# Attention and experts on one core: the softmax shifts turned by VectorE in 32x32 blocks and set in line through memory, in place of TensorE's transposes

## The chip, the cores and the metric

The kernel runs on one core of one Trainium2 chip. Its time is the device time in microseconds (us) of one execution. Five engines of the core matter, each with its own instruction stream: TensorE (PE, with its weight loads PEld), VectorE (DVE), ScalarE (ACT), GpSimd (POOL) and SyncE (SP), which here only waits and issues DMAs. They meet by semaphores.

## The reference

What must be computed, for `x` of shape (4, 2048, 256), float32:

```python
x = x + ln(attn(ln(x)))        # 16 heads of 16, causal
x = x + ln(ffn(ln(x)))         # 8 experts, the 2 best of each batch by its first token

# attn
scores = jnp.where(causal, einsum('bhqd,bhkd->bhqk', q, k) * HD ** -0.5, -inf)
out = einsum('bhqk,bhkd->bhqd', softmax(scores), v)
# ffn
h = gelu(einsum('bsd,bkde->bkse', x, W1[idx]) + b1[idx])
out = sum(einsum('bkse,bkef->bksf', h, W2[idx]) + b2[idx]) / 2
```

## The kernel before, in words

Three stages follow each other. **Stage A** (0 to 207 us) normalises x in 16 chunks of 512 tokens, multiplies by the weights of queries, keys and values, splits queries and keys into three bf16 parts each, and stores all to memory. **Stage B** (207 to 1688 us) is the attention. **Stage C** is the output projection, the layer norms and the experts.

**Stage B's work.** Heads are taken in groups of four, two groups (`g`) in each of eight rounds (`it`). Queries go in four chunks (`c`) of 512, keys in tiles (`kt`) of 128; a *key step* j is one key tile of one chunk of one group, and there are 640. For each step, for each pair of heads (`s`) and each head of the pair (`p`):

- *Scores*, line 1104 (`take_scores`): keys stand still, queries move, two matmuls (`ab`) of up to 512 columns into `psS`. Their contraction takes 64 rows or 33. Heads 0 and 2 use the upper 64 rows of the array (p = 0), heads 1 and 3 the lower 64 (p = 1), and matmuls in different halves run side by side. The 33rd row of the second matmul is a row of ones in `kT` against a row of `qT` that holds each query's *shift*: minus its largest score. So the shift is subtracted inside the matmul.
- *Exponentials*, line 1068, ScalarE: one instruction for two heads.
- *Mask*, line 1039, GpSimd, on tiles at the diagonal.
- *Values*, line 1121 (`take_values`): four heads in float32 into the four 32-column strips of `psO`. One such block uses all 128 rows.

**The maxima.** The shifts must be known before a chunk's first scores. So TensorE computes the scores of a chunk once more, queries standing still, in *units* of up to 512 keys (`multiply`, lines 613 and 615; 613 lays the causal mask down) into a ring of three banks, and VectorE takes each unit's maximum (`reduce`, line 631) and frees the bank. Units with `heads` even use the upper half of the array, odd ones the lower. At the end of a chunk (`ends`) VectorE reduces the parts to `nmax` (line 636): 128 queries by 16 columns (4 heads x 4 tiles). Queries run along partitions there, but the row of `qT` needs them along one partition.

**The turn.** Hence a turn for each chunk, 64 in all, 62 of them in stage B: TensorE transposes `nmax` into a ring bank (line 623), VectorE copies it as bf16 to `nmT` (line 646), and SyncE lays it into rows 32 and 96 of `qT` with four DMAs (`place`, line 653). Scores of the chunk wait for all four (`nm_ld`).

**What sets the order.** `ORDERS` is a string that fixes the order on TensorE for stage B: 0 and 1 are a score matmul for p = 0 or 1, a and b a unit for the upper or lower half, v a block of values, t a turn. VectorE, ScalarE and SyncE walk the same list and pick out their own. The first 54 entries of the list of units (`LEAD`) are done in stage A, two at a time. `PBUF` lets scores run at most four steps ahead of values. SyncE's queue in stage B also holds the loads of the next group (two a step in steps 2 to 14 of each group), and the stores of `outT`.

## Time and profile before

| | |
|---|---|
| median of 3 runs | 2049.87 us (2047.66 to 2054.5) |
| the profiled execution | 2049.51 us |
| its span, first to last instruction | 2047.8 us |
| granted TensorE clock, mean | 0.99 of full speed |
| TensorE busy | 1976.5 us, 97% |
| VectorE busy | 1791.3 us, 87% |
| ScalarE busy | 1363.0 us, 67% |

A busy share is that of an engine over the whole span. Matmuls overlap in the trace, so busy time says that TensorE had something under way, not that it ran at its peak; on TensorE one reads the step from the start of one instruction to the start of the next. A row of weight loads (PEld) that sat idle need not be lost time either, since loads run ahead of matmuls. 1.7 us lie around the span.

### The profile page before, as it was taken

To read this page: it belongs to the slowest core of one execution; us is meant where nothing else is said; L and a number is where in the kernel's file an instruction comes from. 1 tells how busy PE (TensorE), PEld (TensorE's weight loads), DVE (VectorE), ACT (ScalarE), POOL (GpSimd) and SP (SyncE) were. 2 spreads that over 40 slices of the span, in tenths; PEclk is the share of its full clock that TensorE was granted. 3 is DMA by queue.
4 is the path that set the end of the run, shared out by engine and by line. 5 is a ranking of instruction groups with operands and counts; after the bars stand their busy time and mean duration, and the time that the engine had idled before them with its cause. 6 is when DMAs were issued, how large, how long until landed. Compare 5 with 4: busy or idle time off the path is not lost.

```text
span 2047.8 us, 39736 instructions
## 1 busy us (share of the span) xinstructions
PE 1976.5 (97%) x15772; PEld 869.5 (42%) x15772; DVE 1791.3 (87%) x3564; ACT 1363.0 (67%) x1653; POOL 305.4 (15%) x373
## 2 busy tenths in 40 slices
PE   9999999999999999999999999999999996999996
PEld 6655333333333333333333333333333324667664
DVE  6876999999999999989999999999899917898883
ACT  5766757777777777777777777777777781333332
POOL 4333101011010101011010101111010104322000
PEclk9999999999999999999999999999999997999999
DMA  5877515050322304041423505051332034454320
GB/s 171 259 230 202 111 37 101 7 92 22 79 50 49 74 23 91 8 90 27 77 45 51 91 8 90 7 92 34 67 58 41 17 109 113 116 138 112 91 67 31
DMA packets 144907, 162.44 MB, mean 79 GB/s; under 512 B 52946, under 2 KB 118610, under 8 KB 144722
## 3 DMA queue, kind: packets, MB, share of 16 engines
q1 hardware_dynamic: 137554, 147.26, 31.2%
q0 software_dynamic: 7168, 12.64, 2.8%
q8 instruction: 124, 2.03, 0.4%
q14 instruction: 61, 0.50, 0.1%
HBM read 99.77 MB, written 59.77 MB: 78 GB/s over the span
## 4 chain that ended last, share of the span: by engine, by line
PE 81%; DVE 11%; ACT 4%; issue 2%; DMA 1%; SPq 1%; POOL 0%; ACTq 0%; POOLq 0%; DVEq 0%
PE b_psO L1121 25%; PE b_psS L1104 25%; PE b_ring L615 13%; PE a_psQK L906 6%; DVE b_pmax L631 4%; PE c_psH L1501 3%; PE a_psV L918 3%; PE c_psO L1514 3%; ACT b_prob L1068 2%; PE b_ring L613 1%; PE c_psA L1471 1%; DVE c_ln_x_stats L81 1%; DVE c_attn L105 1%; DVE c_ln_f_stats L81 1%; PE a_psT L881 1%
## 5 line engine op out<-in xcount | busy, mean ns | idle before, releaser
L631 DVE TENSOR_REDUCE b_pmax<-b_ring 128x1 f32<-128x512 f32 (+4 forms) x2284 | 1336.7, 648 | 75.1 <-PE b_ring L615 59.2
L1068 ACT ACTIVATE b_prob<-b_psS 128x1024 f32<-128x1024 f32 (+3 forms) x1280 | 1085.2, 895 | 367.3 <-PE b_psS L1104 362.6
L1104 PE MATMUL b_psS<-g_qT,g_kT 64*128 64x512 bf16 (+6 forms) x5120 | 833.2, 347 | 10.1 <-ACT b_prob L1068 7.2
L615 PE MATMUL b_ring<-g_kT,g_qT 64*128 64x512 bf16 (+2 forms) x2500 | 714.5, 348 | 2.9 <-DVE b_pmax L631 1.5
L1121 PE MATMUL b_psO<-b_prob,g_v 128*32 128x512 f32 (+3 forms) x5120 | 595.0, 540 | 0.3
L1104 PEld LDWEIGHTS b_psS<-g_qT,g_kT 64*128 64x128 bf16 (+1 forms) x5120 | 295.4, 94 | 460.6 <-ACT b_prob L1068 343.4
L1039 POOL TENSOR_SCALAR_AFFINE_SELECT b_prob<-b_prob 128x512 f32<-128x512 f32 x256 | 162.7, 636 | 1315.8 <-ACT b_prob L1068 1315.5
L615 PEld LDWEIGHTS b_ring<-g_kT,g_qT 64*128 64x128 bf16 x2500 | 221.2, 94 | 234.2 <-DVE b_pmax L631 162.4
L613 PE MATMUL b_ring<-later,query_of 64*128 64x128 bf16 x988 | 191.9, 219 | 3.0 <-DVE b_pmax L631 2.4
L1121 PEld LDWEIGHTS b_psO<-b_prob,g_v 128*32 128x32 f32 x5120 | 103.4, 108 | 172.1 <-issue 131.9
L1501 PE MATMUL c_psH<-c_yT,c_w1e 128*128 128x512 f32 x256 | 119.4, 613 | 22.0 <-ACT c_hT L1426 21.7
L906 PE MATMUL a_psQK<-c_cc,a_w 128*128 128x512 f32 x256 | 115.8, 599 | 1.2 <-ACT c_cc L833 1.2
L1514 PE MATMUL c_psO<-c_w2e,c_hT 128*128 128x256 f32 x512 | 113.6, 380 | 1.2 <-DMA c_b2e<-in_L_ffn_b 1.2
L613 PEld LDWEIGHTS b_ring<-later,query_of 64*128 64x128 bf16 x988 | 88.1, 94 | 50.3 <-DVE b_pmax L631 23.8
L1514 PEld LDWEIGHTS c_psO<-c_w2e,c_hT 128*128 128x128 f32 x512 | 96.9, 190 | 20.7 <-issue 5.3
L1501 PEld LDWEIGHTS c_psH<-c_yT,c_w1e 128*128 128x128 f32 x256 | 48.5, 194 | 83.2 <-issue 48.1
L1471 PE MATMUL c_psA<-wo,c_cc 128*128 128x256 f32 x256 | 65.6, 415 | 11.8 <-DVE c_attn L1320 7.0
L96 ACT ACTIVATE c_ln_x_std<-c_ln_x_var,eps 128x4 f32<-128x4 f32 x16 | 4.8, 298 | 103.8 <-DVE c_ln_x_var L93 103.8
L1426 ACT ACTIVATE c_hT<-c_psH,c_b1e 128x512 f32<-128x512 f32 x64 | 42.7, 686 | 44.2 <-PE c_psH L1501 44.0
L906 PEld LDWEIGHTS a_psQK<-c_cc,a_w 128*128 128x128 f32 x256 | 47.2, 190 | 54.6 <-issue 54.0
L1471 PEld LDWEIGHTS c_psA<-wo,c_cc 128*128 128x128 f32 x256 | 52.7, 211 | 21.1 <-issue 11.8
L918 PE MATMUL a_psV<-a_w,c_cc 128*128 128x256 f32 x256 | 58.7, 382 | 0.0
(119 smaller groups left out, 1060.5 us busy)
## 6 DMA issues: line engine op xcount, KB each, us to landing
qk_parts<-a_parts SPq DMA_DIRECT2D x64, 384.0 KB, 4.5
g_qT<-qk_parts SPq DMA_DIRECT2D x184, 128.0 KB, 3.9
g_kT<-qk_parts SPq DMA_DIRECT2D x184, 128.0 KB, 5.1
out_sums<-b_outT SPq DMA_DIRECT2D x64, 256.0 KB, 2.4
v_ones<-a_v SPq DMA_DIRECT2D x16, 544.0 KB, 5.8
g_v<-v_ones SPq DMA_DIRECT2D x32, 272.0 KB, 5.3
a_x<-in_L_attn_x SPq DMA_DIRECT2D x16, 512.0 KB, 5.2
c_x<-in_L_attn_x SPq DMA_DIRECT2D x16, 512.0 KB, 7.3
```

Of the source, the lines that this page charges most:

```text
L613: self.nc.tensor.matmul(to[:, w - P:w], consts.query_of[half:half + HALF, :], consts.later[half:half + HALF, :], start=True, stop=False, s ...
L615: ins_ = self.nc.tensor.matmul(to, groups.qT[own, g, h // 2, 0, t * P:(t + 1) * P], groups.kT[own, g, h // 2, 0, pc * CH:pc * CH + w], sta ...
L631: self.nc.vector.tensor_reduce(pmax[:, c % 2].rearrange("p (h t) n -> p h t n", t=TT)[:, heads[0]:heads[-1] + 1:2, qt, pc], bank[:, 0:k * ...
L906: ins_ = nc.tensor.matmul(psQK[:, i % 2], w[:, t, k, m * P:(m + 1) * P], xT[:, n % 2, k], start=(k == 0), stop=(k == KD - 1))
L918: ins_ = nc.tensor.matmul(psV[:, t], xT[:, n % 2, k, t * P:(t + 1) * P], w[:, 2, k], start=(k == 0), stop=(k == KD - 1))
L1039: nc.gpsimd.affine_select(out=tile, in_=tile, compare_op=ALU.is_ge, fill=0.0, base=0, pattern=[[0, HG], [1, P]], channel_multiplier=-1).th ...
L1068: nc.scalar.activation(prob[:, j % PBUF, 2 * s:2 * s + 2, off:CH], psS[:, 2 * s:2 * s + 2, off:CH], ACT.Exp).then_inc(exp_done, 1)
L1104: ins_ = nc.tensor.matmul(psS[:, 2 * s + p, off:CH], kT[own, g, s, ab, kt * P:(kt + 1) * P], qT[own, g, s, ab, c * CH + off:(c + 1) * CH], ...
L1121: ins_ = nc.tensor.matmul(psO[h * VW:(h + 1) * VW, off:CH], vS[:, g, kt, h * VC:h * VC + VW], prob[:, j % PBUF, h, off:CH], start=(kt == 0 ...
L1471: ins_ = nc.tensor.matmul(psA[:, t], cc[:, c, k, t * P:(t + 1) * P], wo[:, k], start=(k == 0), stop=(k == KD - 1))
L1501: ins_ = nc.tensor.matmul(psH[:, i % 2], w1e[:, e, k, m * P:(m + 1) * P], yT[:, k, c], start=(k == 0), stop=(k == KD - 1))
L1514: ins_ = nc.tensor.matmul(psO[:, t], hT[:, e, m, t * P:(t + 1) * P], w2e[:, e, m], start=(i == 0), stop=(i == 2 * KD - 1))
```

## The change

The turn leaves TensorE and its ring bank. `nmax` becomes bf16 with 32 columns, of which 16 stay zero. When a chunk's maxima end, VectorE itself turns `nmax` with one instruction that transposes each 32x32 block in place of its own: it comes out with 32 queries along the free axis, on 128 partitions (4 blocks x 32 columns). `place` then takes two legs. SyncE stores `nmT` to a scratch in memory (`nm_scr`, 128 runs of 64 bytes) so that there each column's 128 queries stand in line, waits until it has landed, and loads from there with two DMAs, one for each half, in place of four. `ORDERS` has no t, and all of it is drawn up anew, so the places of units, scores and values have all moved; the counts of scores and value blocks are the same. The two turns among the first 54 entries make room for two more units in stage A.

```diff
         self.pmax = ctx.enter_context(nc.sbuf_tensor("b_pmax", [P, 2, HG * TT, NC], F32))
-        self.nmax = ctx.enter_context(nc.sbuf_tensor("b_nmax", [P, 2, HG * TT], F32))
-        self.nmT = ctx.enter_context(nc.sbuf_tensor("b_nmT", [HG * TT, 2, P], BF16))
+        self.nmax = ctx.enter_context(nc.sbuf_tensor("b_nmax", [P, 2, BLOCK], BF16))
+        self.nmT = ctx.enter_context(nc.sbuf_tensor("b_nmT", [P, 2, BLOCK], BF16))
+        self.nmax_set = ctx.enter_context(nc.semaphore("b_nmax_set"))
...
+        self.nc.gpsimd.memset(self.nmax[:, :, :], 0.0).then_inc(self.nmax_set, 1)
         self.nc.gpsimd.memset(self.ones[:, :], 1.0).then_inc(self.ones_set, 1)
...
+BLOCK = 32
 GK = sum(TT * (c + 1) for c in range(NC))
 BK = 2 * GK
...
-    jobs, turns = [], []
-    for it in range(NPAIR):
-        for g in range(2):
-            for c in range(NC):
-                for qt in range(TT):
-                    for pc in range(c + 1):
-                        for heads in units(c, qt, pc):
-                            jobs.append(("max", it, g, c, qt, pc, heads))
-                            if turns and turns[0][0] <= len(jobs) - 2:
-                                jobs.append(turns.pop(0)[1])
-                turns.append((len(jobs), ("turn", it, g, c)))
-    return jobs + [turn for _, turn in turns]
+    return [("max", it, g, c, qt, pc, heads) for it in range(NPAIR) for g in range(2) for c in range(NC)
+            for qt in range(TT) for pc in range(c + 1) for heads in units(c, qt, pc)]
...
 ORDERS = (
-    "a1010b0b1b10b011b01010aava110101aa00a0101v010b0101a1b1010bv0b011b011ab0v1a1a0a00101abvb010ba10101av0b011"
...
+    "b0101ab0a101b0101b0101bb0101b1010a0101v10100b011a1010bav1a0b0101a10av1a10b0a1010av1a100a1010bav0b1a1a101"
...
+        self.nm_turned = sem("b_nm_turned")
+        self.nm_stored = sem("b_nm_stored")
 
     @staticmethod
     def bank(r):
...
-    def turn(self, pe, bank, r, it, g, c):
-        self.wait_bank(pe, r)
-        pe.wait_ge(self.nm_done, it * CHUNKS + g * NC + c + 1)
-        self.nc.tensor.transpose(bank[0:HG * TT, 0:P], self.groups.nmax[:, c % 2], self.consts.ident[:, :]
-                                 ).then_inc(self.ring_full, 1)
-
     def reduce(self, v, bank, r, it, g, c, qt, pc, heads, ends):
         pmax, nmax = self.groups.pmax, self.groups.nmax
         k = len(heads)
...
         if ends:
+            n = it * CHUNKS + g * NC + c + 1
             v.wait_ge(self.ring_free, r + 1)
-            self.nc.vector.tensor_reduce(nmax[:, c % 2], pmax[:, c % 2, :, 0:c + 1], AX.X, ALU.max,
+            self.nc.vector.tensor_reduce(nmax[:, c % 2, 0:HG * TT], pmax[:, c % 2, :, 0:c + 1], AX.X, ALU.max,
                                          negate=True).then_inc(self.nm_done, 1)
-
-    def take_turn(self, v, bank, r, it, g, c):
-        v.wait_ge(self.ring_full, r + 1)
-
-        bg, bc = (g, c - 2) if c >= 2 else (1 - g, c + 2)
-        count = (it + (0 if c < 2 and g == 0 else 1)) * 16 * HG
-        if count > 0:
-            v.wait_ge(self.nm_ld[bg][bc], count)
-        self.nc.vector.tensor_copy(self.groups.nmT[:, c % 2], bank[0:HG * TT, 0:P]).then_inc(self.ring_free, 1)
-
-    def place(self, sp, r, it, g, c):
-
-        sp.wait_ge(self.ring_free, r + 1)
-        for h in range(HG):
-            row = h % 2 * HALF + KB
-            sp.dma_start(self.groups.qT[row:row + 1, g, h // 2, 1, c * CH:(c + 1) * CH]
-                         .rearrange("o (q n) -> o q n", n=P),
-                         self.groups.nmT[h * TT:(h + 1) * TT, c % 2, :]).then_inc(self.nm_ld[g][c], 16)
+            if n <= 2:
+                v.wait_ge(self.groups.nmax_set, 1)
+            v.wait_ge(self.nm_done, n)
+
+            bg, bc = (g, c - 2) if c >= 2 else (1 - g, c + 2)
+            count = (it + (0 if c < 2 and g == 0 else 1)) * 16 * 2
+            if count > 0:
+                v.wait_ge(self.nm_ld[bg][bc], count)
+            self.nc.vector.transpose(self.groups.nmT[:, c % 2], nmax[:, c % 2]).then_inc(self.nm_turned, 1)
+
+    def place(self, sp, it, g, c):
+
+        n = it * CHUNKS + g * NC + c + 1
+        sp.wait_ge(self.nm_turned, n)
+        to = self.nm_scr[c % 2]
+        sp.dma_start(to.rearrange("r b n -> b r n"), self.groups.nmT[:, c % 2]).then_inc(self.nm_stored, 16)
+        sp.wait_ge(self.nm_stored, 16 * n)
+        for p in range(2):
+            row = p * HALF + KB
+            sp.dma_start(self.groups.qT[row:row + 1, g, :, 1, c * CH:(c + 1) * CH],
+                         to[0:HG * TT].rearrange("(s p t) b n -> p s (t b n)", p=2, t=TT)[p:p + 1]
+                         ).then_inc(self.nm_ld[g][c], 16)
 
 
...
-                for r, which in leads_of(n):
-                    if which[0] == "turn":
-                        maxima.place(sp, r, *which[1:])
+                for _, (_, it, g, c, *_, ends) in leads_of(n):
+                    if ends:
+                        maxima.place(sp, it, g, c)
...
-            r = LEAD
             summed = []
             for what, *which in ORDER:
                 if what == "max":
-                    r += 1
-                elif what == "turn":
-                    maxima.place(sp, r, *which)
-                    r += 1
+                    it, g, c, *_, ends = which
+                    if ends:
+                        maxima.place(sp, it, g, c)
...
-                    pe.wait_ge(maxima.nm_ld[g][c], (it + 1) * 16 * HG)
+                    pe.wait_ge(maxima.nm_ld[g][c], (it + 1) * 16 * 2)
...
+    nm_scr = nc.dram_tensor("shifts", (2, BLOCK, P // BLOCK, BLOCK), BF16, kind="Internal").ap()
```

In the rows of order below, an instruction is given by its line, what it writes and reads, its shape and the semaphores it waits for. `b_psS` are scores, `b_ring` the units' banks, `b_psO` the values, `b_nm13` and its like say that the shifts of g = 1, c = 3 lie in `qT`.

VectorE before, where the maxima of the last group's first chunk end (`b_pmax` are the units' maxima):

```order
L631 TENSOR_REDUCE b_pmax<-b_ring 128x1 [waits b_ring_full] x3
L631 TENSOR_REDUCE b_pmax<-b_ring 128x2 [waits b_ring_full]
L631 TENSOR_REDUCE b_pmax<-b_ring 128x1 [waits b_ring_full] x23
L636 TENSOR_REDUCE b_nmax<-b_pmax 128x16 [waits b_ring_free]
L631 TENSOR_REDUCE b_pmax<-b_ring 128x1 [waits b_ring_full] x7
L646 CAST b_nmT<-b_ring 16x128 [waits b_nm10,b_ring_full]
L631 TENSOR_REDUCE b_pmax<-b_ring 128x1 [waits b_ring_full] x2
```

VectorE now, at the same place:

```order
L610 TENSOR_REDUCE b_pmax<-b_ring 128x1 [waits b_ring_full] x3
L610 TENSOR_REDUCE b_pmax<-b_ring 128x2 [waits b_ring_full]
L610 TENSOR_REDUCE b_pmax<-b_ring 128x1 [waits b_ring_full] x23
L616 TENSOR_REDUCE b_nmax<-b_pmax 128x16 [waits b_ring_free]
L626 STREAM_TRANSPOSE b_nmT<-b_nmax 128x32 [waits b_nm10,b_nm_done]
L610 TENSOR_REDUCE b_pmax<-b_ring 128x1 [waits b_ring_full] x11
```

The cast of a turned bank, which stood seven units behind the maxima that it belongs to, is gone; a transpose stands right behind `nmax`, and waits for it.

TensorE before, from the last unit of all (its two matmuls into `b_ring` come first) on, with its turn:

```order
L613 MATMUL b_ring<-later,query_of 128x128 [waits b_ring_free]
L615 MATMUL b_ring<-g_kT,g_qT 128x512
L1104 MATMUL b_psS<-g_qT,g_kT 128x512 [waits b_exp_done]
L1104 MATMUL b_psS<-g_qT,g_kT 128x512 x3
L1104 MATMUL b_psS<-g_qT,g_kT 128x384 [waits b_exp_done]
L1104 MATMUL b_psS<-g_qT,g_kT 128x384 x3
L623 MATMUL b_ring<-ident,b_nmax 16x128 [waits b_nm_done,b_ring_free]
L1104 MATMUL b_psS<-g_qT,g_kT 128x384 [waits b_exp_done]
L1104 MATMUL b_psS<-g_qT,g_kT 128x384 x3
L1121 MATMUL b_psO<-b_prob,g_v 32x512 [waits b_exp_done]
L1121 MATMUL b_psO<-b_prob,g_v 32x512 x3
```

TensorE now, from the last unit on:

```order
L598 MATMUL b_ring<-later,query_of 128x128 [waits b_ring_free]
L600 MATMUL b_ring<-g_kT,g_qT 128x512
L1077 MATMUL b_psS<-g_qT,g_kT 128x384 [waits b_exp_done]
L1077 MATMUL b_psS<-g_qT,g_kT 128x384 x3
L1094 MATMUL b_psO<-b_prob,g_v 32x512 [waits b_exp_done]
L1094 MATMUL b_psO<-b_prob,g_v 32x512 x3
L1077 MATMUL b_psS<-g_qT,g_kT 128x384 [waits b_exp_done]
L1077 MATMUL b_psS<-g_qT,g_kT 128x384 x3
L1077 MATMUL b_psS<-g_qT,g_kT 128x256 [waits b_exp_done]
L1077 MATMUL b_psS<-g_qT,g_kT 128x256 x3
L1094 MATMUL b_psO<-b_prob,g_v 32x512 [waits b_exp_done]
L1094 MATMUL b_psO<-b_prob,g_v 32x512 x3
```

The turn, and its wait for `b_nm_done` amid the scores, are gone. From its last unit to the first scores that wait for `b_nm13`, TensorE had 28 score matmuls, a turn and three blocks of values; now it has 24 score matmuls and six blocks.

SyncE before, at the end of stage A (`g_v` are the values that the first scores wait for too, `a_parts` and `a_v` the chunk stores):

```order
L720 DMA qk_parts<-a_parts 128x3x512 [waits a_low_done]
L720 DMA qk_parts<-a_parts 128x3x512 x3
L299 DMA g_v<-v_ones 128x8x68 x2
L715 DMA v_ones<-a_v 128x4x272 [waits a_v_copied]
L720 DMA qk_parts<-a_parts 128x3x512 [waits a_low_done]
L720 DMA qk_parts<-a_parts 128x3x512 x3
L653 DMA g_qT<-b_nmT 1x4x128 [waits b_ring_free]
L653 DMA g_qT<-b_nmT 1x4x128 x3
```

SyncE now, at the same place:

```order
L704 DMA qk_parts<-a_parts 128x3x512 [waits a_low_done]
L704 DMA qk_parts<-a_parts 128x3x512 x3
L633 DMA shifts<-b_nmT 4x32x32 [waits b_nm_turned]
L637 DMA g_qT<-shifts 1x2x512 [waits b_nm_stored]
L637 DMA g_qT<-shifts 1x2x512
L301 DMA g_v<-v_ones 128x8x68 x2
L699 DMA v_ones<-a_v 128x4x272 [waits a_v_copied]
L704 DMA qk_parts<-a_parts 128x3x512 [waits a_low_done]
L704 DMA qk_parts<-a_parts 128x3x512 x3
```

The shifts of the second chunk have moved ahead of the loads of `g_v`, which now wait behind the landing of the store to `shifts`.

## Rows read from the trace of the kernel before

**Rows 1.** The page: each engine's busy time, its share, its instructions.
```profile
PE 1976.5 (97%) x15772; PEld 869.5 (42%) x15772; DVE 1791.3 (87%) x3564; ACT 1363.0 (67%) x1653; POOL 305.4 (15%) x373
```

**Rows 2.** Windows: stretch, then busy time and (instructions) by engine, clock, DMA.
```profile
207.00:320.00 113.00, 107.54 (x938) 39.22 (x939) 107.83 (x190) 75.35 (x91) 13.34 (x19) 0.97 0.31 66
320.00:1605.00 1285.00, 1277.48 (x12142) 470.88 (x12141) 1218.45 (x2165) 969.23 (x1174) 141.36 (x223) 1.00 0.29 54
1605.00:1648.00 43.00, 42.01 (x388) 14.15 (x390) 37.10 (x63) 34.86 (x44) 5.08 (x8) 1.00 0.05 20
1648.00:1688.00 40.00, 37.28 (x329) 8.61 (x325) 0.55 (x3) 32.93 (x40) 5.08 (x8) 1.00 0.42 138
```

**Rows 3.** VectorE by line, 207 to 1648 us: count, busy, mean, idle before.
```profile
L631 DVE TENSOR_REDUCE b_pmax<-b_ring 128x1 f32<-128x512 f32 (+4 forms) x2284 | 1336.7, 648 | 75.1 <-PE b_ring L615 59.2
L646 DVE CAST b_nmT<-b_ring 16x128 bf16<-16x128 f32 x61 | 16.4, 269 | 0.4 <-PE b_ring L623 0.3
L636 DVE TENSOR_REDUCE b_nmax<-b_pmax 128x16 f32<-128x48 f32 (+3 forms) x61 | 12.1, 198 | 2.1
```

**Rows 4.** Timeline of TensorE: a turn behind a value block (start, length).
```profile
228.26 1.06 PE L1121 MATMUL b_psO<-b_prob,g_v 128*32 128x512 f32 x8
229.28 0.27 PE L623 MATMUL b_ring<-ident,b_nmax 128*16 128x128 f32 x1
229.49 0.39 PE L615 MATMUL b_ring<-g_kT,g_qT 64*128 64x512 bf16 x1
```

**Rows 5.** Timeline of TensorE: a turn amid half-array work.
```profile
543.08 0.37 PE L1104 MATMUL b_psS<-g_qT,g_kT 64*128 64x512 bf16 x1
543.38 0.28 PE L623 MATMUL b_ring<-ident,b_nmax 128*16 128x128 f32 x1
543.59 0.39 PE L1104 MATMUL b_psS<-g_qT,g_kT 64*128 64x512 bf16 x1
```

**Rows 6.** Timeline of TensorE: steps of value blocks and of half-array work.
```profile
705.92 1.07 PE L1121 MATMUL b_psO<-b_prob,g_v 128*32 128x512 f32 x8
706.92 0.28 PE L1104 MATMUL b_psS<-g_qT,g_kT 64*128 64x256 bf16 x1
...
711.62 0.39 PE L1104 MATMUL b_psS<-g_qT,g_kT 64*128 64x512 bf16 x2
711.84 0.38 PE L615 MATMUL b_ring<-g_kT,g_qT 64*128 64x512 bf16 x1
```

**Rows 7.** Waits of TensorE's weight loads, 250 to 1640 us: total, times, longest.
```profile
PEld b_ring L615 <- DVE b_pmax L631: 155.4, 384, 0.9
```

**Rows 8.** TensorE's weight loads of the turns, whole run, by line.
```profile
L623 PEld LDWEIGHTS b_ring<-ident,b_nmax 128*16 128x16 f32 x62 | 5.4, 87 | 31.4 <-DVE b_pmax L631 29.3 <-issue 1.3
```

**Rows 9.** Timeline, all engines: the last shifts, their placing, the next scores.
```profile
1648.09 0.22 DVE L636 TENSOR_REDUCE b_nmax<-b_pmax 128x16 f32<-128x64 f32 x1
...
1648.76 0.28 DVE L646 CAST b_nmT<-b_ring 16x128 bf16<-16x128 f32 x1 [0.45 <-PE b_ring L623]
...
1649.07 2.44 SPq L653 DMA_DIRECT2D g_qT<-b_nmT  x4
...
1654.00 1.05 PE L1104 MATMUL b_psS<-g_qT,g_kT 64*128 64x512 bf16 x8 [0.51 <-ACT b_prob L1068]
```

**Rows 10.** DMA issues: count, KB each, median us from issue to landing.
```profile
g_kT<-qk_parts SPq DMA_DIRECT2D x184, 128.0 KB, 5.1
...
g_v<-v_ones SPq DMA_DIRECT2D x32, 272.0 KB, 5.3
...
inverse_sums<-b_pair_sums SPq DMA_DIRECT2D x8, 64.0 KB, 1.6
...
c_b1e<-in_L_ffn_b SPq DMA_DIRECT2D x8, 1.0 KB, 2.6
```

**Rows 11.** Timeline of SyncE's queue before stage B.
```profile
190.39 2.74 SPq L720 DMA_DIRECT2D qk_parts<-a_parts  x4
193.18 2.41 SPq L299 DMA_DIRECT2D g_v<-v_ones  x2
```

More of the change, by code:

```diff
@@ L404, in first_jobs @@
     jobs = max_jobs()
-    return [job if job[0] == "turn" else (*job, not any(other[:4] == job[:4] for other in jobs[r + 1:]))
-            for r, job in enumerate(jobs[:LEAD])]
+    return [(*job, not any(other[:4] == job[:4] for other in jobs[r + 1:])) for r, job in enumerate(jobs[:LEAD])]
 FIRST_JOBS = first_jobs()
@@ L512, in read_orders @@
     jobs = max_jobs()
-    units_of = [[n for n, job in enumerate(jobs) if job[0] == "max" and job[6][0] % 2 == p] for p in range(2)]
-    turns = [n for n, job in enumerate(jobs) if job[0] == "turn"]
+    units_of = [[n for n, job in enumerate(jobs) if job[6][0] % 2 == p] for p in range(2)]
     left = {}
     for job in jobs:
-        if job[0] == "max":
-            left[job[1:4]] = left.get(job[1:4], 0) + 1
+        left[job[1:4]] = left.get(job[1:4], 0) + 1
     for job in jobs[:LEAD]:
-        if job[0] == "max":
-            left[job[1:4]] -= 1
+        left[job[1:4]] -= 1
     order, at, valued = [], [0, 0], 0
     taken = [sum(n < LEAD for n in units_of[p]) for p in range(2)]
-    turned = sum(n < LEAD for n in turns)
     for sign in "".join(ORDERS):
@@ L538, in read_orders @@
             order.append((*job, left[job[1:4]] == 0))
-        elif sign == "t":
-            job = jobs[turns[turned]]
-            turned += 1
-            assert left[job[1:]] == 0
-            order.append(job)
         else:
@@ L547, in read_orders @@
             valued += 1
-    assert valued == len(KEY_STEPS) and turned == len(turns) and not any(left.values())
+    assert valued == len(KEY_STEPS) and not any(left.values())
     return order
@@ L805, in lead @@
                 for r, which in leads(n, k):
-                    if which[0] == "max":
-                        maxima.reduce(v, ring[:, maxima.bank(r)], r, *which[1:])
-                    else:
-                        maxima.take_turn(v, ring[:, maxima.bank(r)], r, *which[1:])
+                    maxima.reduce(v, ring[:, maxima.bank(r)], r, *which[1:])
             normalise(variance(0), 0)
@@ L1048, in _ @@
                     maxima.reduce(v, ring[:, maxima.bank(r)], r, *which)
-                    r += 1
-                elif what == "turn":
-                    maxima.take_turn(v, ring[:, maxima.bank(r)], r, *which)
                     r += 1
@@ L1132, in _ @@
             for what, *which in ORDER:
-                if what in ("max", "turn"):
+                if what == "max":
                     if r == LEAD:
                         pe.wait_ge(stores.v_copied, B * NC)
-                    if what == "max":
-                        maxima.multiply(pe, ring[:, maxima.bank(r)], r, *which)
-                    else:
-                        maxima.turn(pe, ring[:, maxima.bank(r)], r, *which)
+                    maxima.multiply(pe, ring[:, maxima.bank(r)], r, *which)
                     r += 1
```

169 lines of the change are left out of this document (83 added, 86 removed).

## The prediction

> **What bounds the kernel now.** I read the page's first row, then the busy time by stretch, then VectorE by line, then the timeline of TensorE around single turns, then waits and the DMA queue. The page shows TensorE busy 97% of the span [rows 1]. The stretches [rows 2] cut this up; the change works from 207 to 1688 us. From 320 to 1605 TensorE is busy 1277.5 of 1285 us and VectorE 1218.5 (94.8%): two engines near full, with 7.5 and 66.5 us idle. From 207 to 320, the first group, VectorE is busy 107.8 of 113 us and TensorE waits more (107.5): there the reduces set the pace. After 1648 VectorE has nothing left, and ScalarE and TensorE finish alone. So a microsecond saved on TensorE counts in the long middle only as far as VectorE can keep up. It has some room: 75.1 us idle before its reduces, 59.2 of them waiting for TensorE's units [rows 3]. TensorE waits for VectorE too: its weight loads for units stood 384 times for a bank, 155.4 us in sum, most of it under running matmuls [rows 7]. Neither engine alone is the bound; they lean on each other.
>
> **The turns leave TensorE.** Behind a value block, the block takes 1.02 us to the turn's start and the turn 0.21 us to the next start [rows 4]; a like block without a turn takes 1.00 [rows 6]. So 0.21 us each. Amid half-array work the turn comes 0.30 us after its predecessor and gives way after 0.21 [rows 5], where the like step is 0.22 [rows 6]: 0.08 more. In the order string before, 42 of the 62 turns of stage B stand next to a value block, 20 do not. 62 x 0.21 = 13.0, and 20 x 0.08 = 1.6: 14.6 us, the end from below. From above, the weight loads of the 62 turns found their engine idle for 31.4 us [rows 8], 0.51 each, which would all have to be lost time. A turn also holds one of three banks and makes TensorE wait in order for `nmax`, so something of that is lost; I stay near the timelines, with a fifth of the distance: **18.0 us**, 0.29 each.
>
> The Trainium skill has a rule here (TensorEngine Tiling (Array Packing), Key Properties): a change of tiling mode drains the array. Read strictly, each turn would cost its own 0.27 and the drain of its predecessor, 0.17, 62 x 0.44 = 27 us. The rows agree only amid half-array work, and for less; behind value blocks 1.02 against 1.00 shows no drain beyond what a block already pays. By the rule the result would be 9 us lower.
>
> **The halves are filled less evenly.** The new order could give some of this back. Between two value blocks, TensorE needs about as long as the fuller half has columns. Counted over all score and mask and unit matmuls between blocks, the fuller halves hold 1,811,072 columns before and 1,821,056 now; the sum of both halves is the same. At 0.22 us for 512 [rows 6] 9,984 more columns are 4.3 us if the fuller half sets each step. It does so only partly, since other waits cover it; from below it costs nothing. I take **+3**.
>
> **The first group.** There VectorE is the bound, so TensorE's four turns (0.29 x 4) bring nothing by themselves. But until the last value block of that group VectorE takes 173 units in place of 179, counted from both orders; two units went to stage A, where VectorE has room, four to later. At 1336.7 / 2284 = 0.585 us [rows 3] 6 x 0.585 = 3.5, and four casts change for transposes, below, 0.3: **-3.8**. The 58 other turns then count for 18.0 x 58 / 62 = **-16.8**. The last group has 68 units in place of 60, where VectorE has room (37.1 of 43 us [rows 2]) and then nothing.
>
> **VectorE.** 61 casts go, 0.27 each by mean [rows 3]. A transpose of 128x32 bf16 the trace doesn't show. Its nearest rows are the 16-column reduce to `nmax`, 0.20, and the cast, 0.27 [rows 3]; from below half of the former, 0.10, from above twice the latter, 0.54. I take 0.20, with no gap of note before it, since `nmax` itself waits for a reduce in the same way and sat idle 2.1 us over 61 [rows 3]. So VectorE gets 0.07 x 56 = 4 us less to do from 320 to 1605 (from +15 to -10). TensorE wants to be some 13 us quicker there, so VectorE's idle time would shrink from 66.5 to about 57. Less slack means more bank waits; in the trace about 7.5 of TensorE's middle is open idle time with 66.5 of slack, and I give back **+2** (0 to 6). The transpose also stands at once behind its `nmax`; behind it waits the next reduce, and TensorE for its bank, 0.2 us as with the cast.
>
> **The longer way of the shifts.** Now: end of `nmax` to the first issue 0.76 us, four issues to 1651.51, next scores at 1654.00 [rows 9]. New: transpose 0.25 with its wait, issue and landing of the store, issue of two loads (0.6 each, 2.44 / 4 in [rows 9]), landing of the second. A landing isn't shown for such small pieces. Nearest rows: 1.6 us for a 64 KB store, 2.6 for a 1 KB load, 5.1 for a load in the phases when the next group comes in [rows 10]. That makes 0.3 + 1.6 + 0.6 + 2.6 = 5.1 us at best, about 6.5 as I take it, 11 in the loading phases. How much is there? I added the durations of what stands in the new order from a chunk's last unit to its first scores. Of the 62 chunks nine have under 9 us: 3.5, 6.4, 7.0, 7.3, 7.5, 7.8, 7.9, 8.5, 8.7; the other third chunks have 15 and more, second ones 25, first ones 34. All but one are the last chunks of a group, whose maxima end outside the loading phase (steps 2 to 14). The 3.5 stands at the end of the first group, filled with sixteen units that VectorE has to clear first, at 0.585 each, so it is longer than it counts. So 6.5 us costs about **+1** over all (0 to 9 for 9 us).
>
> At the seam of A and B, SyncE's store waits for a landing before the loads of `g_v` are issued: now they go at 193.18 [rows 11]. New: 193.2 + about 5 for a store behind 4 x 384 KB + 1.2 for the loads, 2.4 for the issues, 5.3 to land [rows 10] = 207.1, and the first scores stand at 207.6. **+0.5** (0 to 3).
>
> In SyncE's queue behind the wait for the store stand slices of the next group and `outT` stores. A slice was asked for 9 us and more before its first unit in the old order, and is so in the new one; 128 small issues fewer outweigh the 62 waits. I cost it at nothing.
>
> **The sum.** -16.8 - 3.8 + 3 + 2 + 1 + 0.5 = -14.1. Made against the profiled execution, 2049.5 us: **2035.4**. That execution is within 0.4 of the median, 2049.87. A measurement of this kernel can tell about 0.3%, 6.1 us, from no change.
>
> **Rivals.**
>
> *VectorE is the bound all along* (2039 to 2044). Then TensorE's turns are worth only what VectorE loses with them: 3.8 in the first group and 4 for casts against transposes; -7.8, 2041.7. For it: 94.8% busy and the 384 bank waits. Against: 59.2 us in which VectorE waits for TensorE. 0.19.
>
> *The turns cost more than their slots* (2018 to 2028). A turn holds one of three banks, and TensorE stands in order behind `nmax`. If half of the 31.4 us [rows 8] is lost on top of the 14.6, and VectorE's slack takes nothing back: -30.3 x 58 / 62 = -28.3, with -3.8 + 3 + 1.5 = -27.6, 2021.9; a quarter gives 2029. Against it: TensorE's open idle time is small. 0.12.
>
> *The way through memory is too long* (slower). Price: the sum over the nine chunks, and those that join, of what the way takes beyond their time. At 8 us it is 9, at 9 us 16, at 10 us 25, at 12 us 51 by the same count, less 3 for the first group. From about 9.3 us it eats the whole gain; at 11 us it makes +19, 2069. For it: loads in bulk land in 5.1 [rows 10], so a store plus a load could reach 11 if the queue is never free. Against: these places lie outside the loading phases, and the small transfers shown land in 1.6 to 2.6.
> The Trainium skill speaks for this rival (DMA: Bandwidth & Descriptors, Specifications and Anatomy of one DMA): about 2 us fixed for each transfer, and pieces under 512 B, here 64 B, are read, changed and written back. By its 2 us twice the way is 0.3 + 2 + 0.6 + 0.6 + 2 = 5.5, no loss; no run yet shows what the small pieces add.
>
> *New stalls of the new order* (2044 to 2056, no measurable difference): bank and exponential waits that counts of columns don't show, 10 us of them. 0.10.
>
> **How the numbers follow.** Forecast as summed, 2028 to 2039: 0.52. VectorE bound: 0.19. More gain: 0.12. No difference: 0.10. Slower than 2056, by memory: 0.07. Faster by over 0.3% (below 2043.7): 0.52 + 0.19 + 0.12 = 0.83. The range of 8 in 10 is 2023 to 2047: it leaves out half of the greater gain, some of the case without difference and the slower one. It holds the bounds of turns (14.6, and 31.4 in part) and of the transpose up to +10.
>
> **What would show it.** In the profile after: stage B, first to last score matmul, some 1466 us in place of 1481; the first group's end about 4 us earlier. No full-array matmul among `b_ring`. The transpose at 0.15 to 0.3 us, 62 of them. VectorE's idle before reduces near 65 us rather than 75. From the store's issue to the end of the second load under 7 us, and no open wait of score matmuls for `g_qT` over 1 us but at the seam or the last chunk. I am wrong if TensorE waits for `g_qT` many times, if the transpose takes over 0.5 us, or if bank waits grow by as much as the turns save.

## The result

| | before | after |
|---|---|---|
| median | 2052.59 us (2047.66 to 2059.84, 20 runs) | 2042.11 us (2035.77 to 2049.31, 20 runs) |
| profiled execution | 2049.51 us | 2039.01 us |
| span | 2047.8 us | 2037.3 us |
| stage B, first scores to last value block | 1480.7 us | 1469.2 us |

The changed kernel takes 0.995 of the time before, 95% interval 0.9939 to 0.996: about 10 us faster, where 14 were forecast. The 2035.4 us predicted lie 6.7 below the median, inside the range of 2023 to 2047. Of all executions two, 2074.74 and 2929.76 us, ran in a slower state with a granted clock of 0.939 and 0.607, and every time below is a median without them.

### The profile page after: what moved, and what is told of

Read it like the earlier page. It is cut to its first block and busy times, and to the rows that moved or that the text cites. A ratio compares the mean times of both kernels' runs of the same rounds, so it can differ in the third digit from the quotient of the medians.

```text
span 2037.3 us, 39483 instructions
## 1 busy us (share of the span) xinstructions
PE 1964.9 (96%) x15708; PEld 864.4 (42%) x15708; DVE 1792.2 (88%) x3564; ACT 1362.6 (67%) x1653; POOL 304.6 (15%) x374
## 5 line engine op out<-in xcount | busy, mean ns | idle before, releaser
L610 DVE TENSOR_REDUCE b_pmax<-b_ring 128x1 f32<-128x512 f32 (+3 forms) x2282 | 1330.0, 647 | 64.9 <-PE b_ring L600 51.1
L1077 PE MATMUL b_psS<-g_qT,g_kT 64*128 64x512 bf16 (+7 forms) x5120 | 837.5, 348 | 8.0 <-ACT b_prob L1041 5.7
L600 PE MATMUL b_ring<-g_kT,g_qT 64*128 64x512 bf16 (+3 forms) x2498 | 713.8, 347 | 4.0 <-DVE b_pmax L610 2.5
```

The costliest lines, as they stand in the source:

```text
L600: ins_ = self.nc.tensor.matmul(to, groups.qT[own, g, h // 2, 0, t * P:(t + 1) * P], groups.kT[own, g, h // 2, 0, pc * CH:pc * CH + w], sta ...
L610: self.nc.vector.tensor_reduce(pmax[:, c % 2].rearrange("p (h t) n -> p h t n", t=TT)[:, heads[0]:heads[-1] + 1:2, qt, pc], bank[:, 0:k * ...
L1077: ins_ = nc.tensor.matmul(psS[:, 2 * s + p, off:CH], kT[own, g, s, ab, kt * P:(kt + 1) * P], qT[own, g, s, ab, c * CH + off:(c + 1) * CH], ...
```

## The profile after

The page's first row answers to [rows 1]:

```profile
PE 1964.9 (96%) x15708; PEld 864.4 (42%) x15708; DVE 1792.2 (88%) x3564; ACT 1362.6 (67%) x1653; POOL 304.6 (15%) x374
```

The stretches answer to [rows 2]; columns are the stretch and its length, busy time and (instructions) of TensorE, its weight load, VectorE, ScalarE and GpSimd, then the granted clock, the DMA share and GB/s:

```profile
207.00:320.00 113.00, 108.20 (x930) 39.15 (x930) 105.53 (x184) 75.94 (x90) 14.04 (x19) 0.95 0.32 68
320.00:1605.00 1285.00, 1278.43 (x12204) 469.57 (x12201) 1223.99 (x2180) 980.57 (x1189) 143.74 (x227) 1.00 0.30 55
1605.00:1648.00 43.00, 40.97 (x376) 13.78 (x378) 30.53 (x53) 33.05 (x41) 5.07 (x8) 0.98 0.09 27
1648.00:1688.00 40.00, 31.24 (x240) 9.32 (x237) 5.11 (x3) 25.33 (x29) 11.44 (x8) 0.90 0.38 126
```

From 320 to 1605 us TensorE is as full as before, and VectorE is busy 5.5 us more in the same stretch: 2180 instructions stand there where 2165 did. The stretches are fixed in time, so these sums can't show a gain; the table by groups below does. The clock of the last two stretches, 0.98 and 0.90, is taken up below.

VectorE by line from 207 to 1640 (the reduces' count is that of the whole run) answers to [rows 3]. After the bar stand busy time and mean, then the idle time ahead and who ended it:

```profile
L610 DVE TENSOR_REDUCE b_pmax<-b_ring 128x1 f32<-128x512 f32 (+3 forms) x2282 | 1330.0, 647 | 64.9 <-PE b_ring L600 51.1
...
L626 DVE STREAM_TRANSPOSE b_nmT<-b_nmax 128x32 bf16<-128x32 bf16 x62 | 13.1, 212 | 2.3 <-DVE b_nmax L616 0.2
...
L616 DVE TENSOR_REDUCE b_nmax<-b_pmax 128x16 bf16<-128x48 f32 (+3 forms) x62 | 12.3, 198 | 2.1
```

The transpose, which no row of before showed, takes 0.21 us (taken: 0.20) and hardly waits. VectorE's idle time before reduces fell from 75.1 to 64.9; some 65 was forecast.

TensorE's weight loads from 250 to 1640 us answer to [rows 7]: the unit loads stood 164.8 us for a bank in 398 places, 9 us and 14 places more than before. Most of that lies under running matmuls.

```profile
PEld b_psS L1077 <- ACT b_prob L1041: 330.7, 523, 1.7
PEld b_ring L600 <- DVE b_pmax L610: 164.8, 398, 2.4
```

The new way of the shifts, in the timeline of all engines at the tightest chunk of the run (start, length, instruction), beside [rows 9]:

```profile
1636.42 0.22 DVE L616 TENSOR_REDUCE b_nmax<-b_pmax 128x16 bf16<-128x64 f32 x1
1636.67 0.21 DVE L626 STREAM_TRANSPOSE b_nmT<-b_nmax 128x32 bf16<-128x32 bf16 x1
1636.91 0.55 SPq L633 DMA_DIRECT2D shifts<-b_nmT  x1
...
1638.88 1.14 SPq L637 DMA_DIRECT2D g_qT<-shifts  x2
...
1641.75 0.55 PEld L1077 LDWEIGHTS b_psS<-g_qT,g_kT 64*128 64x128 bf16 x8 [0.20 <-issue]
```

`nmax` ends at 1636.64, the store is issued 0.27 later, the loads 1.97 behind that, and the scores start 5.1 us after `nmax`. Over the 62 chunks of stage B the median from store issue to load issue is 1.96 us, and the longest 2.9. The scores never waited openly for the shifts. Only at the seam with stage A did the store take longer, as SyncE's queue shows (4.0 us from its issue to the loads'); this answers to [rows 11]:

```profile
194.09 1.05 SPq L633 DMA_DIRECT2D shifts<-b_nmT  x1
198.10 1.15 SPq L637 DMA_DIRECT2D g_qT<-shifts  x2
199.29 1.03 SPq L301 DMA_DIRECT2D g_v<-v_ones  x2
```

**Where the time went, by groups.** From the timelines I took, for each of the sixteen groups of stage B, the time from the end of one group's last value block to the end of the next group's. The first group begins with the first scores. Entries are rounded one by one.

| us | start of stage B | first group | 14 middle groups | last group | sum against before |
|---|---|---|---|---|---|
| before | 207.5 | 112.2 | 1285.3 | 83.2 | |
| after | 208.3 | 111.0 | 1273.6 | 84.6 | -10.6 |
| after - before | +0.8 | -1.2 | -11.7 | +1.4 | |

Stage C is equal in both (359.7 and 359.8 us). So the gain is 0.84 us for each middle group; the ends gave some of it back. Of one kernel the middle repeats from execution to execution to 0.3 us (1273.3 to 1273.6 in five executions of the new order, some with a changed last group or a longer store), the first group does not (108.9 to 112.0). The granted clock bears on this: in the middle groups it is 1.00 in every kernel here but the one with three store legs, while all of them lose clock in the first group and in stage C. That makes the middle a finer gauge than the whole time, and the experiments are read on it. For the order of before there is one profiled execution of each kernel, so how well its middle repeats isn't measured.

## Experiments

Each group ran beside the kernel before. "Middle" is the sum over the 14 middle groups in the one execution that was profiled.

### The two halves of the change, one at a time

*New way, old order*: the changed kernel with the string of before, the t's struck out.

```diff
-ORDERS = ( <the new string> )
+ORDERS = ( <the string of before, without t, less the two units that stage A takes> )
```

> The new way of the shifts (VectorE's transpose, the store and two loads) in the order of before, its turns struck out and nothing else moved; the two units that stage A now takes are struck out too. My theory, that TensorE's turns were worth 18 us and the new order gives 3 back in uneven halves and VectorE 2: 12 to 16 us faster than before, so at least as fast as the changed kernel (ratio to before 0.992 to 0.994). Rival A, the gain comes from the new order: within 3 us of before (0.9985 or more). Rival B, VectorE is the bound: 6 to 8 us faster (0.996 to 0.997).

*Old way, new order*: before's turns with the new string, 62 t's put in, 51 of them beside a value block, and the two units back that stage A had taken.

```diff
-ORDERS = ( <the string of before> )
+ORDERS = ( <the new string, with t's and those two units> )
```

> TensorE's turns, cast and four DMAs as before, in the new order of scores, units and values; a turn is put in for each chunk two or more units behind its maxima, 51 of 62 beside a value block. My theory: the order by itself loses 3 us to uneven halves and gains up to 4 in the first group, so within 4 us of before (ratio 0.998 to 1.002). Rival A, the gain comes from the order: 8 us or more faster than before (0.996 or less).

| | time | ratio to before | middle | against before |
|---|---|---|---|---|
| new way, old order | 2053.89 | 1.0002 [0.9988, 1.0016] | 1283.7 | -1.6 |
| old way, new order | 2058.88 | 1.0029 [1.0013, 1.0046] | 1287.1 | +1.8 |
| both (the change) | 2042.11 | 0.995 [0.9939, 0.996] | 1273.6 | -11.7 |

Neither half gives anything alone. In the old order 56 turns taken out of the middle bring 1.6 us, 0.03 each. In the new order the same step brings 13.5 us, 0.24 each. The new order with turns is 1.8 us worse than the kernel before.

The first expectation failed: 12 to 16 us were forecast for the new way in the old order, and the time is that of before; this lies where its rival A had it. The second came out just outside, 1.0029 where 0.998 to 1.002 was given, but its rival A, 8 us from the order alone, failed as well. So neither "the turns are the gain" nor "the order is the gain" holds; it takes both.

Two things limit the comparison. The middle of the new order holds four units fewer (2041 against 2045, by the strings; the last group has eight more), by the prediction's 0.585 us each 2.3 us of VectorE's work at most; the pairs within one order are free of this. And the new order was drawn for a kernel without turns, and the turns were put in afterwards. Whether an order drawn afresh around the turns would gain too, no run tests.

### Is it the slot on TensorE, or the turn's bank and waits?

Bare slots: the same transpose on TensorE, but of a constant, into the bank that the next unit uses, read by nobody; no bank of its own, no wait for `nmax`, no cast. All else is the changed kernel. One run has them in the new order at the places of the run above, one in the old order at the places of before's turns.

```diff
+        elif sign == "t":
+            order.append(("slot",))
...
+                elif what == "slot":
+                    bank = r if r > LEAD else r + 1
+                    maxima.wait_bank(pe, bank)
+                    nc.tensor.transpose(ring[0:HG * TT, maxima.bank(bank), 0:P], consts.ident[:, 0:HG * TT],
+                                        consts.ident[:, :])
```

> The changed kernel with 62 transposes put back on TensorE as bare slots: each turns a constant into the bank that the next unit will use, waits only for that bank, and nobody reads it; they stand where the turns stood in the earlier run with the old way in the new order. VectorE's work, the way of the shifts and the order of all else are the changed kernel's. Theory A (the 0.2 us slot is itself what a turn costs once the order is drawn without it): the 14 middle groups lose about 13 us, 0.24 each, the kernel is at 2055. Theory B (the slot lies beside other work; what costs is that a turn holds one of three banks, makes TensorE wait for nmax and VectorE for the cast): middle groups lose under 4 us, 2043 to 2046. Between: the loss divides.

> The same bare slots in the order of the kernel before, at the very places where its turns stood, with the new way of the shifts. The run without slots in that order took 2053.9. Theory A (a slot costs its length): 2053.9 + 13 = 2067. Theory C (the old order was drawn around its turns, so slots at those places cost next to nothing, 0.03 to 0.08 us each): 2055 to 2059, middle groups 1285 to 1288.

| middle, us | turns (bank, `nmax` wait, cast) | bare slots | nothing |
|---|---|---|---|
| old order | 1285.3 | 1288.8 | 1283.7 |
| new order | 1287.1 | 1284.4 | 1273.6 |

Times: new order with slots 2053.61 (1.0009 [0.9991, 1.0027]), 13.1 us over the changed kernel's 2040.52 on the same chip; old order with slots 2057.95 (1.0019 [1.0001, 1.0037]), 4.1 over the run without. The two runs in the old order were made on different chips; their ratios to before, 1.0002 and 1.0019, have intervals that overlap, and the 5.1 us in the middle is what tells them apart. In the new order a bare slot costs 10.8 / 56 = 0.19 us, which is its length: a timeline of TensorE behind a value block, and the slots as a group from 320 to 1605 us.

```profile
569.23 1.06 PE L1095 MATMUL b_psO<-b_prob,g_v 128*32 128x512 f32 x8
570.23 0.28 PE L1115 MATMUL b_ring<-ident 128*16 128x128 f32 x1
570.44 0.39 PE L1078 MATMUL b_psS<-g_qT,g_kT 64*128 64x512 bf16 x1
```

```profile
L1115 PE MATMUL b_ring<-ident 128*16 128x128 f32 x56 | 15.5, 277 | 0.0
```

Block start to slot 1.00, slot to the next start 0.21, where the turn of before in [rows 4] had 1.02 and 0.21. A slot also waits for the next unit's bank, ahead of its place; but TensorE sat idle 0.0 us before all 56, so this wait is not what costs. So theory A held in the new order: the slot itself costs, and a real turn with its bank, wait and cast takes 2.7 us more in the middle, 0.05 each. In the old order a slot costs 5.1 / 56 = 0.09, somewhat over the 0.03 to 0.08 expected. That it fills time there in which TensorE would have stood for something else is the likely reading, but not shown. And before's real turns at those very places were 3.5 us better than bare slots, the other way round than in the new order; so the 2.7 us are not a price of bank, wait and cast that could be carried over. A real turn shifts the bank of every later unit by one, a slot doesn't, and no run separates that.

### What more of either engine costs

*Each turn three times on TensorE, in the kernel before*, and *each transpose three times on VectorE, in the changed kernel* (`TURNS` is 3 in both):

```diff
-        self.nc.tensor.transpose(bank[0:HG * TT, 0:P], self.groups.nmax[:, c % 2], self.consts.ident[:, :]
-                                 ).then_inc(self.ring_full, 1)
+        for _ in range(TURNS):
+            ins_ = self.nc.tensor.transpose(bank[0:HG * TT, 0:P], self.groups.nmax[:, c % 2], self.consts.ident[:, :])
+        ins_.then_inc(self.ring_full, 1)
```
```diff
+            for extra in range(TURNS - 1):
+                self.nc.vector.transpose(self.groups.spare[:, extra], nmax[:, c % 2])
             self.nc.vector.transpose(self.groups.nmT[:, c % 2], nmax[:, c % 2]).then_inc(self.nm_turned, 1)
```

> The kernel before with each turn's transpose done three times on TensorE into the same bank: 124 more slots in stage B, nothing more on VectorE. My theory, TensorE's slots set the time: 124 x 0.21 = 26 us at full price, at least 18, so 2068 to 2079 by ratio 1.009 to 1.013. Rival B, VectorE is the bound and TensorE has slack: 8 us or less (ratio 1.004 or less).

> The changed kernel with each of VectorE's transposes done three times (two go to a spare tile): 124 x 0.21 = 26 us more on VectorE in stage B, nothing more on TensorE. Rival B, VectorE is the bound: 22 to 26 us slower than the changed kernel. My theory, the two engines lean on each other: 8 to 16 us slower, since VectorE's 65 us of idle time take up part of it. If VectorE had real room, under 3 us.

The additions turned out shorter than expected. On TensorE three in a row took 0.43 us to the next start, and a lone one takes 0.21 [rows 4], so each added one is 0.11:

```profile
548.50 0.37 PE L1106 MATMUL b_psS<-g_qT,g_kT 64*128 64x512 bf16 x1
548.81 0.50 PE L625 MATMUL b_ring<-ident,b_nmax 128*16 128x128 f32 x3
549.24 0.39 PE L1106 MATMUL b_psS<-g_qT,g_kT 64*128 64x512 bf16 x1
```

On VectorE three in a row take 0.32 us to the start of the next reduce:

```profile
543.15 0.22 DVE L618 TENSOR_REDUCE b_nmax<-b_pmax 128x16 bf16<-128x64 f32 x1
543.41 0.30 DVE L629 STREAM_TRANSPOSE b_spare<-b_nmax 128x32 bf16<-128x32 bf16 x2
543.64 0.17 DVE L630 STREAM_TRANSPOSE b_nmT<-b_nmax 128x32 bf16<-128x32 bf16 x1
543.73 2.79 DVE L612 TENSOR_REDUCE b_pmax<-b_ring 128x1 f32<-128x128 f32 x7
```

A lone one, in the changed kernel, is recorded as 0.21 long, but the next reduce starts 0.14 behind its start, so each added one is 0.09:

```profile
541.74 0.21 DVE L626 STREAM_TRANSPOSE b_nmT<-b_nmax 128x32 bf16<-128x32 bf16 x1
541.88 2.80 DVE L610 TENSOR_REDUCE b_pmax<-b_ring 128x1 f32<-128x128 f32 x7
```

| | added in the middle | middle | share paid | time, ratio to before |
|---|---|---|---|---|
| TensorE, old order | 112 x 0.11 = 12.3 us | 1292.9, +7.6 | 0.6 | 2062.39, 1.0045 [1.0027, 1.0064] |
| VectorE, new order | 112 x 0.09 = 10.1 us | 1279.1, +5.5 | 0.5 | 2047.46, 0.9977 [0.9965, 0.9988] |

The whole times fell short of both expectations, 18 us or more and 8 to 16 us, because half as much was added as they had counted on; the ratio of the first, 1.0045, stands at the edge of what the rival "VectorE is the bound" allowed. The share paid decides in its place: work on either engine is paid for in part. That rules out VectorE as the bound all along, in the new order at least: some 10 us more on it cost 5.5, and the change gained 11.7 in the middle, where that rival allowed 4.

### How much room the way through memory has

The store leg is made twice or three times, each waited for: 1.96 us more, or 3.9. The edit for two; for three both 2s are 3s.

```diff
-        sp.dma_start(to.rearrange("r b n -> b r n"), self.groups.nmT[:, c % 2]).then_inc(self.nm_stored, 16)
-        sp.wait_ge(self.nm_stored, 16 * n)
+        for leg in range(2):
+            sp.dma_start(to.rearrange("r b n -> b r n"), self.groups.nmT[:, c % 2]).then_inc(self.nm_stored, 16)
+            sp.wait_ge(self.nm_stored, 16 * (2 * (n - 1) + leg + 1))
```

> The changed kernel with the store of the shifts done and waited for twice: the way of the shifts is 1.96 us longer for each chunk. In the trace of the changed kernel the first scores stand 5.1, 6.1, 6.2, 6.6, 6.7, 6.8, 7.3, 7.3, 7.6 us behind the shifts at the nine tightest chunks, and none waits, so the way takes at most 5.1. My theory: it becomes 7.1 at most, and costs 0 to 5 us. Rival, the way already sets the starts of chunks: 9 x 1.96 = 18 us.

> As the one with two stores, with three: the way is 3.9 us longer, 9.0 at most. My theory: the sum of what nine chunks then lack is 22 us, so 12 to 24 us slower than the changed kernel. Rival, that the way sets the starts already: 35 us. If there is more room than I read: under 6 us.

With two legs the open waits of TensorE for a DMA are these (total, times, longest):

```profile
PE b_psS L1078 <- DMA g_qT<-shifts: 1.6, 2, 1.4
```

Stage B took 1468.5 us, as without the extra leg; the time is 2045.88, 0.997 [0.9955, 0.9985]. The last chunk, the tightest, now waits openly and so shows how long the way is:

```profile
1633.22 0.22 DVE L616 TENSOR_REDUCE b_nmax<-b_pmax 128x16 bf16<-128x64 f32 x1
1637.62 1.19 SPq L638 DMA_DIRECT2D g_qT<-shifts  x2
1640.01 0.82 PE L1078 MATMUL b_psS<-g_qT,g_kT 64*128 64x512 bf16 x6 [1.39 <-DMA g_qT<-shifts]
```

From the end of `nmax` to the scores it is 6.6 us, 4.6 without the added leg: that is the way of the changed kernel, half a microsecond under its tightest chunk. With three:

```profile
PE b_psS L1078 <- DMA g_qT<-shifts: 17.1, 9, 3.3
PE b_ring L598 <- DMA g_v<-v_ones: 8.6, 4, 2.5
```

Stage B took 1506.0 us, the time is 2076.12, 1.0103 [1.0054, 1.0152]. From `nmax` to scores the tight chunks now take 8.5 to 9.2 us, and nine waits show, 17.1 us in sum; the prediction had counted nine chunks under 9 us, and 16 us of loss at 9 us. The second row is another effect: four times the first unit of a new group waits for that group's loads, 8.6 us. They stand in SyncE's queue behind the legs; with two legs and in the changed kernel no such wait is open. That is 25.7 of the 36.8 us by which stage B grew; the mean clock of this execution was 0.979 where the changed kernel's was 0.989, and most of the rest would fit that, though no run separates it. The whole time is 34 us over the changed kernel's, outside the 12 to 24 expected and near the 35 of the rival in which the way had set the starts all along; that rival is refuted by the two legs, which cost stage B nothing where it had 18 us. The prediction's own rival, a way through memory that is too long, was real, between 2 and 4 us away.

### The clock at the end, and a try at more

In the last group of the changed kernel three value blocks stand in a row, and behind them TensorE runs out of exponentials. Its timeline (in brackets: idle time and who ended it):

```profile
1641.75 1.04 PE L1077 MATMUL b_psS<-g_qT,g_kT 64*128 64x512 bf16 x8
1643.54 0.61 PE L1077 MATMUL b_psS<-g_qT,g_kT 64*128 64x512 bf16 x4 [0.74 <-ACT b_prob L1041]
1644.45 0.61 PE L1077 MATMUL b_psS<-g_qT,g_kT 64*128 64x512 bf16 x4 [0.30 <-ACT b_prob L1041]
1645.37 0.61 PE L1077 MATMUL b_psS<-g_qT,g_kT 64*128 64x512 bf16 x4 [0.31 <-ACT b_prob L1041]
1645.91 1.94 PE L1094 MATMUL b_psO<-b_prob,g_v 128*32 128x512 f32 x8
1647.78 1.80 PE L1077 MATMUL b_psS<-g_qT,g_kT 64*128 64x512 bf16 x8
1649.51 1.07 PE L1094 MATMUL b_psO<-b_prob,g_v 128*32 128x512 f32 x8
```

After three gaps (0.74, 0.30, 0.31 us) the value block at 1645.91 takes 1.94 us where the next takes 1.07: the clock has gone to its lower level, 1.2 GHz, for some 3.5 us. I set the three blocks apart:

```diff
-v00010111vvv10101010001111001010v
+v00010111v10101010v0011v11001010v
```

> The changed kernel, but the three value blocks that stand in a row before the last chunk's first scores are spread between those scores. My theory: TensorE had too little to do there (it waits for exponentials from 1641 to 1646 us) and its granted clock fell for 3.4 us behind it; spread, the blocks fill these waits and the fall after 1646 is gone: 1 to 3 us faster than the changed kernel. Rival: the fall comes wherever it comes, and the time is that of the changed kernel within 1 us.

Windows of the changed kernel (granted clock in the third place from the end), then of this one:

```profile
260.00:280.00 20.00, 18.91 (x151) 7.32 (x148) 17.85 (x37) 8.06 (x12) 1.90 (x3) 0.83 0.04 11
280.00:300.00 20.00, 17.40 (x142) 5.35 (x136) 16.84 (x28) 13.37 (x14) 0.00 (x0) 0.91 0.03 9
1640.00:1660.00 20.00, 17.52 (x136) 3.70 (x128) 0.00 (x0) 15.23 (x18) 0.63 (x1) 0.91 0.54 167
```

```profile
260.00:280.00 20.00, 19.20 (x160) 8.03 (x156) 18.41 (x38) 9.13 (x12) 1.57 (x3) 0.83 0.05 16
280.00:300.00 20.00, 17.34 (x147) 5.40 (x146) 18.33 (x31) 14.47 (x15) 0.00 (x0) 1.00 0.11 35
1640.00:1660.00 20.00, 18.39 (x146) 3.84 (x144) 0.00 (x0) 17.70 (x20) 0.00 (x0) 1.00 0.56 166
```

The later fall is gone and the last group takes 83.0 us in place of 84.6; the fall at 280 to 300 is absent in this execution too, and its first group takes 108.9. The time was 2040.71, 0.9942 [0.9922, 0.9962]. Beside the changed kernel on one chip:

> The changed kernel itself once more, to stand on the same chip beside the next run: 2042 by the earlier runs, 0.995 of the kernel before.

> The changed kernel with the three value blocks that stood in a row in the last group set apart, once more, now beside the changed kernel on the same chip. If the fall of TensorE's clock at the end comes from the stretch in which TensorE waited behind those three blocks, it is faster by about 1.5 us; if that fall comes and goes by itself, the two agree within 1 us.

2040.52 (0.994 [0.9919, 0.9961]) and 2042.14 (0.9942 [0.9923, 0.9961]). The last group was again 84.6 and 82.9 us, with the fall of the one at the same place as before and none in the other. In three further kernels with the same row of three (three transposes, two store legs, and bare slots in the new order) the last group has a fall of the same length too, but some 20 us later, and with the turns in that order there is none. So setting the blocks apart removes the fall, in two executions of two; that the gaps at 1643 bring it is likely, not shown. The first group came out at 110.8 and 112.0, and the whole time can't tell the two kernels apart: the 1.5 us expected did not show in it. No version here is shown to beat the changed kernel.

## Why the prediction was right

The number lies in its range and most terms came out near their sizes, but one premise was missing, and without it the same sum fails for half of the change.

**Which bound.** Right: two engines lean on each other. Both added work on TensorE and added work on VectorE cost a part of their length.

**The turns (-16.8 outside the first group).** The price per turn was 0.29; with the order fixed as the new one, taking them away measured 0.24, of which a bare slot alone costs 0.19. The sum for 56 turns is 13.5 where the step had 16.2, less the 2 given back for VectorE's slack: 14.2. This step stands, and its lower end (the slot from the timeline, 0.21) was nearest. What the prediction did not see is that this price belongs to the new order. In the order of before the same removal brings 0.03 each, most likely since that order had been filled around its turns. It added the terms as if they were independent; they are right only in the sequence "new order first, then the turns out". By the same terms it forecast 12 to 16 us for the new way in the old order, and nothing came. That the sum came out for the whole change is in part luck: it was asked for the one combination in which it holds.

**Uneven halves (+3).** The new order with turns was +1.8 in the middle, near the term; but that is all that the order does, and no run isolates the halves. With the turns out the same order, with its fuller halves, is 10.1 us faster in the middle than the old one. So the count of columns doesn't rank orders by itself, and the mechanism stays open.

**First group (-3.8).** Here the sum went wrong most: -1.2 in the profiled execution. The count of VectorE's work isn't what failed. In two executions of the new order with as much time at the lower level in that group as before had, 6.8 us, it takes 108.9, that is -3.3. With 10.2 us at that level it takes 110.8 and 111.0, with 13.6 us 112.0, whether in a longer fall or in a second one. The windows above show it for the profiled one, 0.91 against 1.00 from 280 to 300. In the new way with the old order the same stretch is worse still, and the first group takes 116.6:

```profile
260.00:280.00 20.00, 18.51 (x135) 7.76 (x133) 16.71 (x36) 8.07 (x11) 1.36 (x3) 0.74 0.05 16
280.00:300.00 20.00, 16.26 (x120) 4.54 (x124) 16.54 (x28) 12.14 (x13) 0.00 (x0) 0.87 0.01 1
```

So the step that was mis-sized is "6 x 0.585 = 3.5, and four casts: -3.8": it took the clock there as given, and a second fall in that group returned most of it in the execution that was profiled. What sets off the falls in the first group no run shows.

**VectorE (0.20 for the transpose, idle to 65).** 0.21 and 64.9. Right. Durations overlap there, though: from start to next start (medians) `nmax` and the cast took 0.12 and 0.30, `nmax` and the transpose 0.24 and 0.14, so the exchange gives 0.04 us for each chunk and not 0.07.

**The rule weighed against the turns.** The Trainium skill says that a change of tiling mode drains the array (TensorEngine Tiling (Array Packing), Key Properties). Read strictly, with the prediction's estimate of 0.44 for a turn, the change would have been worth 9 us more. The bare slots measured 0.19, 51 of 62 of them behind a value block: no drain shows beyond what such a block pays anyway.

**The way of the shifts (+1, about 6.5 us).** The way is 4.6 us by the run with two legs, under the 5.1 called best, and cost nothing. The landing of the store took at most 1.96, not 1.6 by the nearest row; the second load, where it was waited for, 1.8 from its issue to the scores in place of 2.6. The Trainium skill (DMA: Bandwidth & Descriptors, Anatomy of one DMA) gives about 2 us as the fixed cost of a transfer, for DMAs issued from GpSimd. This case's trace, on SyncE's queue, agrees for the store with its 1.96, and nothing on top of it shows for pieces of 64 bytes. The chunk counted at 3.5 us, at the end of the first group, had 6.1, as the prediction had warned; nine chunks under 9 us were counted, and nine waits opened with three legs. SyncE's queue, costed at nothing, did cost nothing; it starts to between two legs and three.

**The seam (+0.5).** +0.8, but no cause can be read from it: in ten executions with the new way's stage A the first scores start between 206.0 and 208.4 us, before's at 207.5. The store took 4.0 us where 5 was taken.

**The sum.** Of the 3.5 us between -14.1 and -10.6 the first group holds 2.6 and the seam 0.3. The rest, middle and last group together, was forecast at -10.8 and came out at -10.3: the last group's +1.4 was in no term; without the fall of the clock, as with the blocks set apart, it is -0.2. The other 3 us between forecast and median lie in the level: the 3 runs of before that were shown had a median of 2049.87, twenty had 2052.59. Compared at the same mean clock, as the last section does, the two kernels are 13.5 us apart.

## What to carry to other kernels

A hand-drawn order can be fitted to the very instructions in it. Here taking one kind away and leaving the order gained 0.03 us for each, and keeping the instructions in an order drawn without them gained nothing; only both together paid. Price such a change with the new order fixed and the old mechanism put into it, by bare slots if need be, and don't expect either half alone to pay. When moving a small hand-over off a shared engine onto a slower path, count the chunks whose room is near the path's length; here the count gave the number of chunks that waited once the path was 8.5 us long.

## What the runs showed of the hardware

Twenty executions of the changed kernel ran from 2035.77 to 2049.31 us, and their mean granted TensorE clock tells them apart: 0.990 for the fastest, 0.984 for the two slowest (2048.39 and 2049.31), about 2.2 us for each 0.001. The kernel before had 0.989 in the mean over the 71 executions beside the experiments, the changed one 0.987 over 27. At the same clock, 0.988, the medians are 2053.4 (10 executions) and 2039.9 (7): 13.5 us, nearly the sum that was forecast. So of the 14 us forecast about 3 went to a lower mean clock; that the change itself lowers it isn't shown, beyond the fall in the last group.

Several small transposes in a row cost less than a lone one: on TensorE 0.11 against 0.21 us, on VectorE 0.09 against 0.14 from one start to the next, where the record of a lone one is 0.21 long. Multiplying an operation to price it must therefore be read from the added time in the trace, not from the length of one.
